# One core, a two-layer block with a routed expert stage at the end: where three gated products of the last stage run, and how its last sequence is stored

## What is computed

```python
def _layer_norm(x, gamma, beta):
    mu = jnp.mean(x, axis=-1, keepdims=True)
    var = jnp.mean(jnp.square(x - mu), axis=-1, keepdims=True)
    return (x - mu) * jax.lax.rsqrt(var + LN_EPS) * gamma + beta
...
tgt2 = jnp.einsum('bsed,bse->bsd', o, router_w)
return _layer_norm(tgt + tgt2, gamma, beta)
...
x = x + gb * _L1_ffn_ref(h, ...)
return x
```

## Time and profile before

| | us |
|---|---|
| median of three runs | 572.94 (572.18 to 574.33) |
| the profiled execution | 574.9 |
| its span, first to last instruction | 573.0 |
| last stage, from the first bn_stats to the last addition | 546.26 to 568.17 |
| the last loaded sum complete in PSUM | 560.19 |
| last store issued | 568.20 |

### The profile page before, as it was taken

How to read it: one execution, slowest core, us unless ns; L and a number is a source line. 1 busy time by engine, 2 the same in 40 slices (tenths; PEclk the granted TensorE clock), 3 DMA queues, 4 the chain that set the end, 5 groups by cost and what they waited for, 6 DMA issues and landing times.

```text
span 573.0 us, 12147 instructions
## 1 busy us (share of the span) xinstructions
PE 507.9 (89%) x3328; PEld 420.9 (73%) x3328; DVE 438.5 (77%) x1651; ACT 352.2 (61%) x944; POOL 280.6 (49%) x349
## 2 busy tenths in 40 slices
PE   5799999999999999988999999515999999999991
PEld 3467888888888887756777777414999999989630
DVE  3758898989898989977899999853666666656375
ACT  3978787787878584544656666312566666555354
POOL 3144363535353535410266666770666666666323
PEclk9989999999999999999999999855999999999996
DMA  9299999999100000006511111111122222222293
GB/s 279 85 290 176 178 165 179 165 173 185 61 19 15 6 18 2 21 18 194 152 44 39 39 38 44 44 58 45 57 72 68 76 72 68 61 72 67 80 278 112
DMA packets 76386, 54.70 MB, mean 95 GB/s; under 512 B 10524, under 2 KB 69408, under 8 KB 76184
## 3 DMA queue, kind: packets, MB, share of 16 engines
q1 hardware_dynamic: 70352, 43.39, 38.4%
q0 software_dynamic: 4320, 8.99, 4.7%
q10 hardware_dynamic: 1640, 1.45, 0.8%
HBM read 40.62 MB, written 31.58 MB: 126 GB/s over the span
## 4 chain that ended last, share of the span: by engine, by line
PE 62%; DVE 22%; ACT 6%; issue 5%; DMA 2%; DVEq 1%; SPq 0%; POOL 0%; ACTq 0%
PE bank L1817 10%; PE bank L1834 10%; PE bank L678 5%; PE bank L680 5%; PE bank L679 5%; PE bank L789 4%; DVE nmx L1471 2%; PE bank L724 2%; PE bank L809 2%; PE bank L735 2%; PE bank L785 2%; PE bank L794 2%; PE bank L1710 2%; PE bank L720 1%; DVE arena L1607 1%
## 5 line engine op out<-in xcount | busy, mean ns | idle before, releaser
L1307 POOL DMA_INDIRECT results<-arena x71 | 74.2, 1045 | 60.6 <-ACT arena L1395 55.7
L1817 PE MATMUL bank<-front,arena 128*128 128x128 f32 x568 | 77.9, 281 | 2.7 <-DVE arena L1607 1.4
L1265 POOL DMA_INDIRECT queue<-arena,pos x64 | 62.6, 979 | 28.1 <-issue 14.1
L1834 PE MATMUL bank<-h_all,front 128*128 x568 | 75.7, 277 | 0.1
L1817 PEld LDWEIGHTS bank<-front,arena 128*128 128x128 f32 x568 | 70.6, 195 | 5.7 <-issue 4.5
L292 POOL TENSOR_TENSOR arena<-arena,half_neg 128x1 f32<-128x1 f32 x32 | 19.7, 616 | 110.2 <-ACT arena L458 110.2
L1834 PEld LDWEIGHTS bank<-h_all,front 128*128 128x128 f32 x568 | 69.6, 193 | 0.3 <-issue 0.2
L1607 DVE COPY arena<-arena 128x516 f32 x71 | 36.6, 515 | 40.4 <-issue 37.3
L1389 ACT ACTIVATE front<-bank 128x128 f32<-128x128 f32 x71 | 19.7, 278 | 60.9 <-PE bank L1810 42.9
L678 PE MATMUL bank<-h_hi,wc_hi 128*128 128x512 f32 x96 | 45.1, 470 | 1.3 <-ACT arena L439 1.3
L1618 DVE TENSOR_SCALAR front<-bank,arena 128x128 f32<-128x128 f32 x142 | 42.8, 342 | 2.9 <-PE bank L1817 2.6
(11 more groups left out here) (295 smaller groups left out, 1393.1 us busy)
## 6 DMA issues: line engine op xcount, KB each, us to landing
queue<-in_pad_rows SPq DMA_DIRECT2D x8, 2178.0 KB, 34.8
arena<-queue SPq DMA_DIRECT2D x71, 66.0 KB
rows<-mod_rows SPq DMA_DIRECT2D x8, 384.0 KB, 6.3
x_keep<-x SPq DMA_DIRECT2D x8, 256.0 KB, 2.3
arena<-in_w SPq DMA_DIRECT2D x1, 2048.0 KB, 9.1
h_all<-in_w SPq DMA_DIRECT2D x1, 2048.0 KB, 7.9
h_all<-results SPq DMA_DIRECT2D x8, 256.0 KB, 4.8
arena<-results SPq DMA_DIRECT2D x8, 256.0 KB, 5.2
```

The lines of the kernel that those rows point to most:

```text
L1265: pool.indirect_dma_start(k.queue, bass.IndirectOffsetOnAxis(ap=pos[:, s, i, c0 + j:c0 + j + 1], axis=0), row[:, s * NC + c0 + j, i, :], N ...
L1307: pool.indirect_dma_start(k.results, bass.IndirectOffsetOnAxis(ap=xg[:, c, D:D + 1].bitcast(I32), axis=0), yw[:, c, :], None).then_inc(S[f ...
L1817: mm = t_.matmul(bank[(2 if g < NG // 2 else 6) + p][:, g * P:g * P + P], wc[:, p, g * P:g * P + P], xt[:, p, :], start=True, stop=True)
L1834: mm = t_.matmul(bank[4 + p][:, 0:D], ht[:, p, g * P:g * P + P], w2[:, e, g, :], start=(g == 0), stop=(g == NG - 1))
```

## The change

Three things, all in the last stage.

- The product of sequences 1, 3 and 5 (`by_pool`) is taken from DVE and given to POOL, directly in front of POOL's addition of the same sequence, and raises a semaphore of its own, `f_pg`. POOL's addition then waits for that one. ACT's wait for the buffer `nn` and POOL's wait in front of the addition go through `weighted(e, b)`, which picks the right semaphore. `join(b)` on DVE returns at once for these three.
- The last sequence is weighed and added on DVE in two halves of two chunks: product, addition, product, addition. The first product waits for two of the four activations only.
- The last sequence is stored in two halves of 128 KB, each on its half of the additions.

`f_pg` counts on a semaphore of an earlier stage that is out of use. The wait for all of `gg` stays at the first product on DVE.

```diff
+        by_pool = (1, 3, 5)
+
+        def weighted(e, b):
+
+            if b >= 0:
+                on_pool = b in by_pool
+                wait(e, "f_pg" if on_pool else "f_g", sum(1 for i in range(b + 1) if (i in by_pool) == on_pool))
...
             for b in range(NB):
                 if b < NB - 1:
                     wait(sp, "f_x2", b + 1)
+                    sp.dma_start(ov[:, b * NC:(b + 1) * NC, :], x[:, b * NC:(b + 1) * NC, :]).then_inc(S["e_out"], 16)
                 else:
-                    wait(sp, "f_x3", 1)
-                sp.dma_start(ov[:, b * NC:(b + 1) * NC, :], x[:, b * NC:(b + 1) * NC, :]).then_inc(S["e_out"], 16)
-            sp.wait_ge(S["e_out"], 16 * NB)
+                    for half in range(2):
+                        wait(sp, "f_x3", half + 1)
+                        sp.dma_start(ov[:, b * NC + 2 * half:b * NC + 2 * half + 2, :],
+                                     x[:, b * NC + 2 * half:b * NC + 2 * half + 2, :]).then_inc(S["e_out"], 16)
+            sp.wait_ge(S["e_out"], 16 * (NB + 1))
...
             for b in range(NB - 1):
-                wait(pool, "f_g", b + 1)
+                if b in by_pool:
+                    wait(pool, "f_x2", b - 1)
+                    wait(pool, "f_n", NC * (b + 1))
+                    g.tensor_tensor(ng[:, b % 2], nn[:, b % 2], over_chunks(gg[:, b, :]), ALU.mult).then_inc(S["f_pg"], 1)
+                weighted(pool, b)
                 g.tensor_tensor(x[:, b * NC:(b + 1) * NC, :], x[:, b * NC:(b + 1) * NC, :], ng[:, b % 2], ALU.add).then_inc(S["f_x2"], 1)
...
-                wait(act, "f_g", b - 1)
+                weighted(act, b - 2)
...
             def join(b):
                 q = b % 2
-                wait(dve, "f_n", NC * (b + 1))
-                wait(dve, "f_gg", NB)
+                if b in by_pool:
+                    return
+                if b == 0:
+                    wait(dve, "f_gg", NB)
                 wait(dve, "f_x2", b - 1)
-                v.tensor_tensor(ng[:, q], nn[:, q], over_chunks(gg[:, b, :]), ALU.mult).then_inc(S["f_g"], 1)
-                if b == NB - 1:
-                    wait(dve, "f_g", b + 1)
+                if b < NB - 1:
+                    wait(dve, "f_n", NC * (b + 1))
+                    v.tensor_tensor(ng[:, q], nn[:, q], over_chunks(gg[:, b, :]), ALU.mult).then_inc(S["f_g"], 1)
+                else:
                     wait(dve, "f_x", NB)
-                    v.tensor_tensor(x[:, b * NC:(b + 1) * NC, :], x[:, b * NC:(b + 1) * NC, :], ng[:, q], ALU.add).then_inc(S["f_x3"], 1)
+                    for half in range(2):
+                        c0, c1 = 2 * half, 2 * half + 2
+                        wait(dve, "f_n", NC * b + c1)
+                        v.tensor_tensor(ng[:, q, c0:c1], nn[:, q, c0:c1], over_chunks(gg[:, b, :], 2), ALU.mult).then_inc(S["f_g"], 1)
+                        wait(dve, "f_g", NB - len(by_pool) + half)
+                        v.tensor_tensor(x[:, b * NC + c0:b * NC + c1, :], x[:, b * NC + c0:b * NC + c1, :], ng[:, q, c0:c1], ALU.add).then_inc(S["f_x3"], 1)
```

More of the change, by code:

```diff
@@ L1027, in layer1 @@
             "q_mr", "q_pos", "q_wa", "q_w0", "q_w1", "q_lg", "f_cnt"))
-    k.retired = k.retired_late
+    k.retired = k.retired_late + [("c_gate", 5)]
     k.sems((), counting_on=(
             "x_t", "x_ev", "w_cp", "h_mm", "ht_a", "ht_d", "y_mm", "y_ev", "y_sc",
-            "t_sum", "f_stats", "f_mv", "f_ve", "f_rs", "f_nm", "f_n", "f_x", "f_gg", "f_g", "f_x2", "f_x3"))
+            "t_sum", "f_stats", "f_mv", "f_ve", "f_rs", "f_nm", "f_n", "f_x", "f_gg", "f_g", "f_x2", "f_x3", "f_pg"))
     with ExitStack() as ctx:
```

## The result

The changed kernel is slower: the ratio of its time to that of the kernel before is 1.0052, with a 95% interval of 1.0036 to 1.0068 over twenty runs of each (medians 576.35 and 573.57 us). By the ratio that is +3.0 us, between 2.1 and 3.9, where +1.2 was forecast; by the medians it is +2.8. The median lies 0.15 us over the upper end of the range, 576.2, and 2.2 over the forecast of 574.2. Of these 2.2 us some 0.6 is not the change's: the forecast started from 572.94, the median of three runs, and that of twenty is 573.57. From 572.94 the same loss would have ended inside the range; what the forecast had wrong is the size of the loss.

A forecast was written before the change was run, and what follows sets the result against it. The prediction took the last stage to be bound by DVE's 2.11 us turn and its exclusion with POOL; +1.57 (products) - 0.04 (halves) - 0.3 (store) = +1.2 us on 572.94 gave 574.2 us, range 572.2 to 576.2.

The forecast's parts named there:

- That DVE and POOL exclude each other: Last stage: DVE instructions with two on-chip inputs and POOL additions wait for each other, making the three moved products cost +1.57 us.
- The order of the two engines: Behind POOL's addition of 0: DVE's small instruction is let in before POOL's product of 1, at 0.14 us.
- 570.2 for the last addition: Last addition's end if POOL's product of 1 goes ahead of DVE's small instruction at 554.29; total 574.7 us.
- What a turn consists of: Two sequences, between POOL's even additions: 1.26 + 0.14 + 1.28 + 0.14 + 1.26 + 0.55 + 0.08 = 4.71 us, against 4.2 before.
- The end of the sum: End of the kernel: summed to DVE's last addition, 568.17 before and 569.70 after (+1.53 us), then its store.
- 568.64: End of POOL's addition of 6, in us, after waiting until 567.43 for DVE's first half product.
- Halving gives 0.04 back: Last sequence in halves on DVE: +1.53 us with the moved products, instead of +1.57 for those alone.
- the half store 0.3: Last store in halves: final transfer of 128 KB instead of 256 KB saves 0.3 us, bounds 0 and 0.44.
- The new waits cost nothing: Semaphore waits in the last stage hold back nothing; ACT's wait before `nn` of 7 has 0.2 us of cover.
- rival 1: POOL in the last stage: its instructions are as short as 1.09 us, turn 4.19, total 572.8 us; chance 0.17.
- Rival 2: Last stage: busy time decides and the exclusion hardly bites, so the change gains, total 570.8 us; chance 0.10.
- rivals 3 and 4: DVE's small instruction shut out over both POOL instructions: all three times 578.9 us (chance 0.08), once only 575.8 us (0.10).

The follow-up runs named there:

- e5: Changed kernel with `nm` made by four DVE instructions of one tensor input each instead of one with two; ratio 1.0042 to the kernel before.
- e6: Changed kernel with a short POOL addition into a spare tile ahead of each moved product; one execution, no ratio, span end 22.23 us after POOL's first addition starts.
- e3: Changed kernel with POOL's product waiting until POOL's own preceding addition is finished; ratio 1.0027 to the kernel before.
- e2: Changed kernel with the three products on POOL but the last sequence weighed, added and stored whole; ratio 1.0048 to the kernel before.
- e9: Changed kernel with the addition of sequence 6 on DVE instead of POOL; ratio 0.9996 to the kernel before.
- e7: Kernel before with the addition of sequence 6 on DVE, behind its product; ratio 0.9968 to the kernel before.
- e8: Kernel before plus a 128 x 4 memset on POOL that waits for DVE's last addition; ratio 1.0026 to the kernel before.
- e4: Changed kernel with only the product of sequence 1 on POOL; ratio 1.0014 to the kernel before.

## Why the prediction missed

Two steps failed. The order of the two engines behind POOL's first addition was wrong, and the sum was carried to DVE's last addition and its store instead of POOL's last instruction. In us of the span: 1.23 forecast (1.57 - 0.04 - 0.3), +0.52 for the wrong end, +0.76 for the order and the turn it makes, +0.06 for POOL's addition of 6, which is held a little longer than forecast: 2.57.

- *That DVE and POOL exclude each other on instructions with two inputs in on-chip memory, and that this turns the saved work into a loss:* right. e5 takes the second input away, and the stall goes. The rule of the Trainium skill ("SBUF — State Buffer", "Who interferes with whom") stands as cited, the order of issue included: e6 and e3 show it, with 0.47 and 0.16 us.
- *The order of the two engines:* wrong. From the earlier trace rows it was concluded that DVE is let in wherever POOL has two instructions in a row, and the turn has a gap of 0.14 us between POOL's addition of 0 and its product of 1 in which that happens. In the earlier trace rows DVE had asked 0.24 us ahead of POOL's second instruction, and the 0.14 comes from an instruction that waited for the one ahead of it. The product of 1 doesn't wait for the addition. It is dispatched 0.04 us before the addition ends, 0.00 to 0.01 ahead of the small instruction, three times out of three. So POOL goes first, and the small instruction takes 1.28 us. e3 makes the product wait, and DVE is let in. The turns are 4.91, 5.08 and 4.90 us, 14.89 in place of 14.13. The prediction named this order and gave it 570.2 for the last addition; 17.47 us behind 553.07 is 570.5. Its total for that order, 574.7, was still summed to the wrong end.
- *What a turn consists of:* wrong in its terms. DVE's product of 2 was to be held by POOL's addition of 1 and end 0.55 behind it. It takes 0.69 and comes after the addition is over; the held small instruction has pushed the whole of DVE's next round behind it. Product 1.26 for 1.28 and the gap ahead of the addition, 0.08 for 0.14, are small beside that. In 5.08 there are 0.19 us of a bn_stats group of sequence 6 that takes 1.08 instead of 0.89 in the changed kernel, e2, e3, e6 and e9, and not before. Its cause wasn't tried.
- *The end of the sum:* wrong. "The last addition ended at 568.17", plus a store, was not what the span ended with; e7 and e8 show that it is POOL's last instruction. By the prediction's own numbers POOL's addition of 6 was to end at 568.64 instead of 566.89, so its sum should have been +1.75, 574.7 us. (Its 568.64 is itself 0.05 short: 567.43 + 1.26 = 568.69.) With the measured turns it is 2.33 + 0.24 (that addition took 1.50 for 1.26) = +2.57.
- *Halving gives 0.04 back, the half store 0.3:* the order came as predicted (the half addition behind POOL's, 1.37 us). But DVE's end doesn't set the span's, SP being through 2.3 us before it in the kernel before and 2.7 in the changed one, so neither term reaches the end. What does reach it has the other sign: the half product holds POOL's addition of 6 and costs 0.21 us (changed kernel against e2). And the 0.3 rested on nothing else being in flight, while the store of 6, issued at 566.4, was still out when the halves went at 566.8 and 567.5.
- *The new waits cost nothing:* held. ACT went from 6 to 7 with no idle time between, so the wait for the product of 5 was covered.
- *Rivals.* POOL's instructions took 1.26 us, so rival 1 falls. Rival 2 falls with the stalls. The shut-out over two instructions (rivals 3 and 4) didn't happen in any trace, and in e6, where POOL has three in a row, DVE got in behind the first. The forecast's direction was right, and its size too small by more than half; what is left between 2.57 and the measured 3.0 is within the interval, 2.1 to 3.9.

## What to carry to other kernels

Ask first what ends the span, and follow it past the last arithmetic to the closing rows of every engine; an engine that finishes early by its busy rows can still be the last one out. Before moving work from one engine to a neighbour with idle time, list the instructions of both that can't run together, the short ones above all, and see who is dispatched first: here an instruction of 0.16 us took 1.28 because the other engine's was dispatched 0.01 us ahead. If one engine's exit is dear, give its last instruction to another, as e7 does with one addition: -1.9 us by the traces, -1.8 (-1.0 to -2.7) measured.

## What the runs showed of the hardware

- POOL's closing DRAIN ended 5.9 to 6.0 us after the end of its last instruction in all twelve traces, be that an addition of 1.26 us or a memset of 0.10 (e8: 563.77 to 569.7). DVE's took 0.73 and 0.46 us in all, with the addition it waited for. Whether POOL's 6 us depend on its earlier transfers wasn't tried.
- In the last stage an instruction of DVE and one of POOL ran one after the other where both had two inputs in on-chip memory. Where one was dispatched 0.04 us or more ahead, it went first: DVE's half product at 564.85, before POOL's addition at 564.89, which took 1.50 us. Where the two came within 0.02 us, POOL went first in all thirteen cases (changed kernel, e2, e4, e6, e9); whether by the order of asking or by a preference at a tie, no run tells. DVE also gets in between POOL instructions that have no gap (e6). An instruction of DVE with one tensor and a pointer from on-chip memory isn't held (e5: 0.58 us for four beside POOL's product).
- The stores of 128 KB landed in 2.0 and 1.8 us in e9 and in 2.4 and 2.1 in the changed kernel, where they went out closer behind one of 256 KB; those of 256 KB took 2.3 at least.
